# Both halves of a batch's destination products around the first sum, and one comparison ahead of the rescale

## The reference

```
xn = layernorm(x);  h = einsum('ni,hid->nhd', xn, W)
e  = leaky(h[src] . a_src + h[dst] . a_dst)              # slope 0.2
al = exp(min(e - segment_max(e, dst)[dst], 20))
x  = x + (segment_sum(al / sum_dst(al) * h[src], dst)) @ W_out
t  = layernorm(x)
x  = x + t + sum over 8 experts of combine_e * (gelu(t @ w1_e + b1_e) @ w2_e + b2_e)   # best 2
```

## Time and profile before

| | |
|---|---|
| median of 3 runs | 1582.72 us (1581.16 to 1583.31) |
| profiled execution | 1581.73 us, its span 1579.9 us |
| busy, share of the span | PE 90%, DVE 70%, ACT 62%, POOL 53% |
| instructions | 29587 |
| granted PE clock, mean | 0.949 of full speed |

### The profile page before, as it was taken

The page is one execution under the profiler, slowest core; times in us unless marked ns, Lnnn a source line. Parts: engine busy times, 40 slices in busy tenths (PEclk is TensorE's granted clock), DMA queues, the critical chain, the costliest instruction groups (busy, mean ns, idle before and its releaser), DMA issues.

```text
span 1579.9 us, 29587 instructions
## 1 busy us (share of the span) xinstructions
PE 1425.4 (90%) x7327; PEld 1144.5 (72%) x7327; DVE 1099.9 (70%) x3031; ACT 980.4 (62%) x2505; POOL 830.3 (53%) x886
## 2 busy tenths in 40 slices
PE   5916776999999999999999999999999999999998
PEld 3813454677777777877777777777777878787887
DVE  6626674677777777777777777777776777777543
ACT  3715564666767675767676666666666767677732
POOL 1357777555556565656565555555555656551000
PEclk9955776899999999999999999999999999999999
DMA  9564654344343433343434434343434343463000
GB/s 225 138 191 133 180 143 133 104 110 116 101 118 103 120 103 113 105 119 106 116 108 112 112 109 114 109 113 108 114 101 116 96 129 94 127 90 61 1 17 17
DMA packets 89788, 174.83 MB, mean 111 GB/s; under 512 B 22455, under 2 KB 56049, under 8 KB 89593
## 3 DMA queue, kind: packets, MB, share of 16 engines
q0 software_dynamic: 40448, 111.89, 28.1%
q1 hardware_dynamic: 48071, 60.77, 12.6%
q10 hardware_dynamic: 1106, 0.27, 0.1%
HBM read 159.24 MB, written 14.43 MB: 110 GB/s over the span
## 4 chain that ended last, share of the span: by engine, by line
PE 65%; issue 10%; ACT 10%; DVE 5%; ACTq 3%; POOL 1%; DMA 0%; DVEq 0%; POOLq 0%
PE agg_ps L1117 22%; PE ob L1192 17%; PE hb L1146 13%; ACT acc L1333 4%; ACT agg_ps L1336 2%; PE ob L1223 2%; PE ob L1146 2%; PE ob L1258 2%; PE kbank L1079 2%; ACTq L654 1%; ACT hT L1365 1%; POOL ring L740 1%; DVE ring L848 1%; PE kbank L1095 1%; PE ob L1198 1%
## 5 line engine op out<-in xcount | busy, mean ns | idle before, releaser
L740 POOL DMA_INDIRECT ring<-table,srcE x832 | 798.3, 959 | 549.3 <-PE agg_ps L1117 309.8
L1117 PE MATMUL agg_ps<-ring,oh 128*128 128x260 f32 x1664 | 562.7, 431 | 59.0 <-ACT agg_ps L1336 41.0
L1333 ACT COPY acc<-agg_ps x831 | 307.7, 370 | 194.7 <-PE agg_ps L1117 130.1
L1192 PE MATMUL ob<-w_sb,hT 128*125 128x256 f32 x1600 | 410.3, 381 | 1.6
L1117 PEld LDWEIGHTS agg_ps<-ring,oh 128*128 128x128 f32 x1664 | 294.7, 201 | 128.5 <-issue 100.9
L1336 ACT COPY agg_ps<-zc 128x260 f32 x832 | 314.6, 378 | 98.6 <-ACT acc L1333 3.2
L1192 PEld LDWEIGHTS ob<-w_sb,hT 128*125 128x125 f32 x1600 | 297.6, 189 | 53.6 <-issue 9.5
L848 DVE TENSOR_TENSOR ring<-ring,kbank 128x1024 f32<-128x1024 f32 x208 | 244.7, 1214 | 50.6 <-ACT ring L1355 50.4
L1365 ACT ACTIVATE hT<-hb,b_sb 128x375 f32<-128x375 f32 (+1 forms) x272 | 154.1, 566 | 157.9 <-PE hb L1146 157.0
L983 DVE SCALAR_TENSOR_TENSOR y<-ob,cmb,y 125x256 f32<-125x256 f32 x400 | 188.9, 475 | 48.3 <-PE ob L1192 44.3
L785 DVE TENSOR_TENSOR oh<-kbank,relE 128x512 f32<-128x512 f32 x208 | 141.6, 681 | 100.5 <-PE kbank L1079 100.5
(11 more groups left out here) (271 smaller groups left out, 1378.4 us busy)
## 6 DMA issues: line engine op xcount, KB each, us to landing
OT<-relb_d SPq DMA_DIRECT2D x52, 512.0 KB
ring<-table,srcE POOLq DMA_INDIRECT x832
y<-in_x_dram SPq DMA_DIRECT2D x50, 125.0 KB
out_dram<-y SPq DMA_DIRECT2D x50, 125.0 KB
table<-hrow SPq DMA_DIRECT2D x25, 227.5 KB
acc<-in_x_dram SPq DMA_DIRECT2D x2, 1568.0 KB
acc<-in_L_ffn_w_dram SPq DMA_DIRECT2D x1, 2048.0 KB, 12.6
w_sb<-in_L_ffn_w_dram SPq DMA_DIRECT2D x1, 2048.0 KB
```

Of the source, the lines that this page charges most:

```text
L740: pool.indirect_dma_start(out=rings[b % RING][:, k, :], out_offset=None, in_=table[:, :], in_offset=bass.IndirectOffsetOnAxis(ap=srcE[:, t ...
L1117: T.matmul(aggf[:, bass.ds(bank_of[k // 8][k % 8], ROW)], oh[:, (4 * b + q) % OHQ, k % 4, :], rings[b % RING][:, k, :], start=False, stop= ...
L1192: t = T.matmul(o[0:Q, 0:D], hT[:, e % 2, f, cols], w2_sb[:, e, f, :], start=f == 0, stop=f == KC - 1)
L1333: A.copy(accf[:, bass.ds(row_of[h][k % 8], ROW)], aggf[:, bass.ds(closed[h][k % 8], ROW)]).then_inc(S["ev"], 1)
```

## The change

On PE, both halves of D come in slot 0, the first ahead of the sum of tile 0 and the second at the end of the slot; the read of block addresses for the second half moves from slot 0 to slot 10 and is done a batch earlier; both reads for batch 0 come ahead of the loop. On DVE, quad 2 is compared ahead of the rescale.

```
 if k == 15:
+    onehot(b, 2)
     if b >= 1:
         rescale(b)
-    onehot(b, 2)
...
 def ahead(it, k):
-    if k in (0, 1) and it + 1 < NBAT:
-        d_of_edges(it + 1, k)
     if k == 0 and it + 1 < NBAT:
-        blocks_of_tiles(it + 1, 1)
+        d_of_edges(it + 1, 1)
+    if k == 10 and it + 2 < NBAT:
+        blocks_of_tiles(it + 2, 1)
     elif k == 12 and it + 2 < NBAT:
         blocks_of_tiles(it + 2, 0)
...
+blocks_of_tiles(0, 1)
 blocks_of_tiles(0, 0)
 for it in range(-1, LAST):
     p, s0 = place(it)
     for k in range(BT):
         s = s0 + k
         if s in FIRST:
             products(p, s)
+        if k == 0 and it + 1 < NBAT:
+            d_of_edges(it + 1, 0)
         edges(it, k)
```

## The result

The changed kernel takes 1541.38 us (median of 4 runs, 1539.49 to 1541.86), the kernel before 1582.28 in the same comparison (1581.16 to 1583.31): a ratio of 0.9739, 95% interval 0.9723 to 0.9756. The direction and most steps were right; about half of the gain was forecast.

A forecast was written before the change was run, and what follows sets the result against it. PE, partly its instruction stream, was taken as the bound; 1.38 us a cycle over 14.7 cycles (20.3 us) plus 1 us for batch 6 made 21 us, giving 1562 us on the median, range 1549 to 1579.

The forecast's parts named there:

- the head of batch 6: Start of batch 6, where less is queued beside it: an estimated gain of 1 us.
- tile 1, and slot 1: Batch heads: tile 1 moves by -0.61, +0.29, +0.16 us; slot 1 loses its second half, 0.20, 0.42, 0.20 us.
- my 2.55: Batch head: tile 1 starts 2.55 us after the comparison ends, from 0.30, 0.84, 0.33 and 1.08 us.
- A: Head kind s = 0, first of three alternating; DVE's idle time takes the comparison, tile 2 comes 0.81 us earlier.
- C: Head kind s = 32, third of three alternating; tile 1 0.16 us later, tile 2 0.04 us earlier.
- B: Head kind s = 16, second of three alternating; tile 1 0.29 us later, tile 2 0.13 us earlier.
- Rival 4: Nothing moves: the address load shows in slot 10 instead, 0.58 us a head; 1583 to 1588 us, chance 0.09.
- rivals 1 and 3: 1: slower issue of 16 products, 1575 to 1580 us, chance 0.10; 3: ACT passes late tile 0 on, 1615, 0.06.
- rival 2: Halves of D run queued at 0.025 us a product, 1525 us, or partly, 1540 to 1551; chance 0.07 together.
- the sequencer, once ahead, hides small things in slots 2 and 3: PE's instruction stream, slots 2 and 3: 0 to 0.3 us a cycle gained, taken as 0.1.
- 0.30 for eC: Slot 3: PE's transpose no longer waits for eC, gaining 0.10 us in B and 0.20 in C.
- at full clock: One 200 us window: PE busy 193.14 us at full clock; no term for clock loss in the forecast.

The follow-up runs named there:

- the kernel with both halves behind tile 0: Changed kernel with both halves of D after the sum of tile 0: 1580.76 us, ratio 0.9951; run again, 1580.10 us.
- widened twin of the kernel before: Kernel before with destination products of 132 columns for 12, on a slow chip: 1730.58 us, ratio 1.0002.
- The comparison alone: Kernel before with only quad 2's comparison moved ahead of the rescale: 1599.2 us, ratio 1.0054.
- the comparison back: Changed kernel with quad 2 compared behind the rescale again: 1599.37 us, ratio 1.0061.
- the read put back: Changed kernel with one more PE address read (banks) behind the second half of D in slot 0: 1585.58 us, ratio 0.9993.
- Slot 14: Changed kernel with quad 2 compared in slot 14, ahead of the last message: 1538.43 us, ratio 0.9697; run again, 1537.63 us.
- both halves ahead: Changed kernel with quad 2 compared in slot 14 and both halves of D ahead of the sum of tile 0: 1549.08 us, ratio 0.9779.
- its wide twin: Changed kernel with both halves of D behind tile 0, products streaming 132 columns for 12: 1565.55 us, ratio 0.9875; slow chip, 1722.87 us.

## Why the prediction was half right

**Right: nothing before batch 7.** Its tile 0 comes 0.4 us later, not earlier, so the 1 us that I took for the head of batch 6 was not there. DVE's wait for rstd in batch 5 took up what was won, as said; the same row of after:

```profile
DVE xn L920 <- POOL rstd L748: 11.0, 1, 11.0
```

**Right, but 6 us too small: tile 1, and slot 1.** Against tile 15 of the batch before, tile 1 moved by -0.75, +0.28 and -0.02 us (medians) for -0.61, +0.29 and +0.16; the second half leaves slot 1 at 0.21, 0.42 and 0.20 for 0.20, 0.42 and 0.20. Together 1.37 us a cycle, 0.98 forecast. (The 1.6 us from tile 0 to tile 1 that I named as the sign in the profile was a slip: my own working gives 1.08.) From the end of the comparison to tile 1 there are 2.49, 2.56 and 2.55 us for my 2.55; what was missing lies mostly ahead of it, where in A and C the comparison starts 0.08 us before the marked end of the work before it and not 0.06 behind. That 2.55 and 1.08 fit is in part luck, since they are made up otherwise than I had them. The first product comes 0.48, 0.42 and 0.86 us behind the comparison, not 0.30, and the first half then takes 0.61, 0.71 and 0.22 us from its first product to its eighth, not 0.84: 0.09 and 0.10 us apart in A and B, and queued in C (0.03). The 1.07 is 0.54 for the sum and then eight products in 0.60 us, (0.60 - 0.17) / 7 = 0.061 us apart, not nine steps of 0.12. The Trainium skill, "TensorE: Matmul & The Clock Gate", Back-to-back issue gap, has about 62 ns where ucode decodes small matmuls; the 0.061 of the second half agrees with it, the first half of A and B is slower.

**Right: slot 10 hides the load, slot 0 does not.** Moving the read alone gave 18 us of the middle; putting one back cost 0.62 to 0.67 us a head; two in slot 10 cost nothing locally. Rival 4 falls, rivals 1 and 3 too: ACT passed nothing on, slots 4 to 15 kept their times although tile 0 comes later against tile 15 by up to 1.04 us. The part of rival 2 (the first half queued in C, 1540 to 1551) named the time, and C's first half is indeed queued. But it starts 0.56 us later than I had it and tile 1 comes at my 2.55 all the same, so that this is not where the gain came from; the halves did not run queued in A and B.

**Wrong, the mis-sized term: "the sequencer, once ahead, hides small things in slots 2 and 3 ... I take 0.1", with 0.30 for eC.** These 0.40 us a cycle measured 0.28 + 0.24 + 0.47 = 0.99 in the medians, and 12.4 us over the 44 batches for 5.9 (from batch 37 on the step gains less). I priced the wait for eC by the idle time marked there: 0.20 in C, none in B and A. In truth the transpose stood at that wait in all three: it starts 0.05 to 0.06 us behind the end of eC. The time shows as matmuls further apart, with no idle marked: in B 0.09 us behind tile 2, 0.12 ahead of the transpose and 0.03 behind it; in A 0.08, 0.20 and 0.02. Delaying eC alone by 1.15 us raised 2 to 3 by 1.13, 0.66 and 0.18 us and added 29 us to the middle, with no other edit. So what pays in slot 3 is that eC comes earlier, which the earlier end of D brings: in B and C until eC no longer holds PE, in A until DVE's own work holds eC.

**Wrong, a term that was missing: TensorE's clock.** I wrote "at full clock" from one window and left it there. The kernel before has four stretches at half clock in the middle, the changed one none in either profile: 6 us. That more work in the products removes nine such stretches and 14 us shows the cause for the kernel with both halves behind tile 0, and there for the seven that stand behind the products; on the two slow chips widened kernels kept some. Three of the four of the kernel before stand behind the routing products of 8 columns, which the change doesn't touch and which stand in the changed kernel too. Why none is left there (heads with less waiting around them) is argued, not shown; the widened twin of the kernel before ran only on a slow chip, and moved nothing. The Trainium skill, "TensorE: Matmul & The Clock Gate", HAM oscillation, puts a fall of the clock down to gaps in which PE idles. The trace here agrees only in part: in the head shown the longest marked idle ahead of the fall is 0.50 us, and what stands between is sixteen products of 12 columns that the profile counts as a busy PE.

**The sum made again,** over the 44 batches of the middle, from the starts of the sums in both traces, the steps with a stretch set apart:

| part | forecast, us | measured, us |
|---|---|---|
| from tile 15 to tile 2 | 0.98 x 14.7 = 14.4 | 20.4 |
| tile 2 to tile 3 | 0.40 x 14.7 = 5.9 | 12.4 |
| tile 3 to tile 15 | 0 | 1.2 |
| TensorE's clock | 0 | 6.3 |
| batch 6 | 1 | -0.4 |

That is 21 forecast and 40 measured, in the trace; the medians differ by 41.

**Misses in the experiments' expectations.** The comparison alone, the comparison back, the read put back, eC late and the address read alone came out 4 to 14 us above what I expected, in part by stretches that I had not priced. Slot 14 came out 20 us above, since I had all three heads run queued, and both halves ahead 45 us. The kernel with both halves behind came out in its range, its wide twin 2.5 us faster against it than expected; of its seven stretches behind tile 0 four stand in A, where B was expected to have most. On the slow chips the kernel before had 15 stretches where 2 to 12 were expected, and its wide twin ten for 0 to 3.

## What to carry to other kernels

A wait that empties PE's queue can cost more than the idle marked at it. Look whether the matmul starts right behind the end of what it waits for (here 0.05 to 0.07 us), compare the starts of the same matmuls where they are queued (here 0.33 us from one to the next) and where they are not (0.45 and 0.54), and price the wait by the difference of the steps. Then look what holds the awaited instruction next: in A it was DVE's own queue, which left 0.29 us to win. A scalar load on PE costs its 0.59 us only where the queue holds less than that; put it where PE has run under long matmuls for a while, and put small products where PE would wait anyway, split around a large one. When a change lengthens or uncovers a run of very small matmuls, look at the granted clock in windows of a few us around it, since a page in 40 slices does not show falls of a few us.

## What the runs showed that I had not expected

- TensorE fell to 1.2 GHz behind runs of small matmuls that the profile counts as a busy PE (eighteen of 8 columns in 2 us, sixteen of 12 in 1.8 us), without a long idle gap. Products widened from 12 to 132 columns made a kernel faster, 1565.55 for 1580.10 us, as nine stretches at half clock went.
- One fall of the clock costs 1.5 to 1.6 us here, and a kernel had from none to 15 in its middle. The kernel before ran from 1581.0 to 1597.4 us in one group of 25 runs, the changed one from 1539.5 to 1541.9 in four. The spread fits a number of stretches that differs from run to run, but only profiled executions show their number, so this is a guess.
- The same kernel took 1587 to 1588 us on three chips and 1731 and 1733 on two others, with the added time at fixed places of the program, behind waits of ACT and DVE that only the profiles of these two chips have. The cause stays open.
